# Second attention of an audio tower: exponentials taken from the score banks head by head, with the negated maximum as bias

## The reference, cut to what matters

```
q = (v @ WQ).reshape(B, S, H, C)
k = (v @ WK).reshape(B, S, H, C)
val = (v @ WV).reshape(B, S, H, C)
scores = jnp.einsum('bshc,bthc->bsth', q, k) * SCALE
A = jax.nn.softmax(scores, axis=2)
u = jnp.einsum('bsth,bthc->bshc', A, val).reshape(B, S, H * C)
return u @ Wout + bout
```

## Time and profile before

| | us |
|---|---|
| median of 3 runs | 961.59 (961.02 to 964.46) |
| the profiled execution, its own time | 963.74 |
| its span, first to last instruction | 962.0 |
| TensorE busy | 914.2 |
| VectorE busy | 703.5 |
| ScalarE busy | 639.6 |
| GpSimd busy | 520.0 |
| first scores of the second attention to its last | 583.46 to 848.13 |

### The profile page before, as it was taken

The page is one execution under the profiler, slowest core; times in us unless marked ns, Lnnn a source line. Parts: engine busy times, 40 slices in busy tenths (PEclk is TensorE's granted clock), DMA queues, the critical chain, the costliest instruction groups (busy, mean ns, idle before and its releaser), DMA issues. The chain is left out here.

```text
span 962.0 us, 35426 instructions
## 1 busy us (share of the span) xinstructions
PE 914.2 (95%) x12664; PEld 665.5 (69%) x12664; DVE 703.5 (73%) x1984; ACT 639.6 (66%) x1214; POOL 520.0 (54%) x815
## 2 busy tenths in 40 slices
PE   8899987999698999999999998999999999989998
PEld 3455655777476888888888884666666666558887
DVE  6677656777466668878878777988888888975553
ACT  2356566888567677868777776777777777743444
POOL 0010126887583687887878876555655556462110
PEclk9899998999899999999999999999999999999999
DMA  7533000000000000000000000000000000000001
GB/s 162 169 67 98 1 1 2 1 0 1 1 1 2 2 3 2 0 0 0 0 0 0 1 3 1 2 2 0 0 0 0 0 0 0 2 2 20 20 22 29
DMA packets 10657, 14.82 MB, mean 15 GB/s; under 512 B 8864, under 2 KB 9120, under 8 KB 9760
## 3 DMA queue, kind: packets, MB, share of 16 engines
q1 hardware_dynamic: 10400, 13.36, 5.7%
q10 hardware_dynamic: 192, 0.59, 0.2%
HBM read 11.85 MB, written 2.10 MB: 15 GB/s over the span
## 5 line engine op out<-in xcount | busy, mean ns | idle before, releaser
L1909 ACT ACTIVATE e_hid<-ps,cst 128x512 f32<-128x512 f32 x256 | 155.2, 689 | 53.0 <-PE ps L1671 53.0
L1606 POOL TENSOR_TENSOR e_acc<-e_acc,e_part 128x512 f32<-128x512 f32 x96 | 122.3, 1274 | 34.3 <-DVE e_part L1837 27.5
L1683 PEld LDWEIGHTS ps<-ew,e_hid 128*64 128x64 f32 x4096 | 124.8, 138 | 21.9 <-issue 10.4
L1683 PE MATMUL ps<-ew,e_hid 128*64 128x64 f32 x4096 | 133.8, 224 | 0.0
L1671 PE MATMUL ps<-e_xs,ew 64*128 64x256 f32 x1024 | 128.1, 389 | 0.7 <-ACT e_hid L1909 0.7
L1837 DVE TENSOR_TENSOR e_part<-ps,e_wt 128x512 f32<-128x512 f32 x128 | 86.8, 687 | 44.5 <-PE ps L1683 38.8
L1671 PEld LDWEIGHTS ps<-e_xs,ew 64*128 64x128 f32 x1024 | 93.5, 186 | 16.2 <-issue 3.1
L2114 POOL TENSOR_TENSOR a_sum<-a_part 128x256 f32<-128x256 f32 x64 | 47.0, 734 | 87.0 <-DVE a_part L2224 86.9
L2184 PEld LDWEIGHTS ps<-cst,a_ex 128*128 128x128 f32 x512 | 55.1, 140 | 49.1 <-issue 49.1
L2213 DVE TENSOR_REDUCE a_rmax<-ps 128x8 f32<-128x1024 f32 x64 | 78.2, 1222 | 14.8 <-PE ps L2176 13.5
L2216 DVE TENSOR_TENSOR a_diff<-ps,a_rmax 128x1024 f32<-128x1024 f32 x64 | 78.4, 1225 | 2.9
(11 more groups left out here) (275 smaller groups left out, 1986.4 us busy)
## 6 DMA issues: line engine op xcount, KB each, us to landing
x_in<-x_dram SPq DMA_DIRECT2D x12, 384.0 KB, 6.2
cst<-cst_dram SPq DMA_DIRECT2D x1, 3101.0 KB, 15.4
out_dram<-e_res SPq DMA_DIRECT2D x16, 128.0 KB, 2.0
ew<-ew_dram SPq DMA_DIRECT2D x1, 1024.0 KB, 8.5
x_in<-x_dram SPq DMA_DIRECT2D x5, 192.0 KB, 5.0
x_in<-x_dram ACTq DMA_DIRECT2D x3, 192.0 KB, 4.5
ew<-ew_dram SPq DMA_DIRECT2D x1, 512.0 KB, 9.3
cst<-cst_dram SPq DMA_DIRECT2D x1, 448.0 KB, 8.8
```

What stands on the lines that cost most here:

```text
L1606: eng.tensor_tensor(acc[:, :, :, :], acc[:, :, :, :], part[n % RING][:, :, :, :], ALU.add).then_inc(sum_sb.sem, 1)
L1683: mm = eng.matmul(m.ps[rows, 6 + n % 2, to:to + C], hid[e % 8][:, a:a + C], w2[:, e * C:e * C + C], start=True, stop=True)
L1909: nc.scalar.activation(hid[e % 8][:, :].rearrange("p (r t) -> p r t", r=2), m.ps[:, 4 - 2 * (n % 2):6 - 2 * (n % 2), j * 256:(j + 1) * 256 ...
```

## The change

The tile `diff` and its subtraction go. The maxima are written negated (`negate=True`), into two buffers in turn. ScalarE takes the exponential of each head by itself, straight from the score banks, with the head's negated maximum as bias: eight instructions of 128 x 128 elements in place of one of 128 x 1024. TensorE's next scores now wait for the last of these eight, where they waited for the subtraction. ScalarE's order of parts becomes `now, x0, lag1, x1, x2`: the exponentials stand ahead of the copy of the piece and of the copy of the transposed matrices, where they stood behind both.

```
-    rmax, rec = sb("rmax", [P, H]), sb("rec", [P, H])
+    nmax, rec = [sb(f"nmax{b}", [P, H]) for b in range(2)], sb("rec", [P, H])
...
         def now(g, b, s):
             if s == 0:
                 eng.wait_ge(uv_sb.sem, uv_sb.at(g, 2))
-                eng.wait_ge(diff_sb.sem, diff_sb.at(g - 1))
+                eng.wait_ge(exp_sb.sem, exp_sb.at(g - 1))
             else:
-                eng.wait_ge(diff_sb.sem, diff_sb.at(g, s))
+                eng.wait_ge(exp_sb.sem, exp_sb.at(g, H * s))
...
         def lag1(g, b, s):
             eng.wait_ge(prob_sb.sem, prob_sb.at(g, s) if s else prob_sb.at(g - 1))
-            eng.wait_ge(exp_sb.sem, exp_sb.at(g, s + 1))
+            eng.wait_ge(exp_sb.sem, exp_sb.at(g, H * (s + 1)))
...
-            eng.tensor_reduce(rmax[:, :], src, AX, ALU.max).then_inc(max_sb.sem, 1)
-            eng.wait_ge(max_sb.sem, max_sb.at(g, s + 1))
-            eng.wait_ge(exp_sb.sem, exp_sb.at(g, s) if s else exp_sb.at(g - 1))
-            eng.tensor_tensor(diff[:, :, :], src, bc(rmax[:, :], [P, H, P]), ALU.subtract).then_inc(diff_sb.sem, 1)
+            eng.tensor_reduce(nmax[s % 2][:, :], src, AX, ALU.max, negate=True).then_inc(max_sb.sem, 1)
...
         def now(g, b, s):
-            eng.wait_ge(diff_sb.sem, diff_sb.at(g, s + 1))
+            eng.wait_ge(max_sb.sem, max_sb.at(g, s + 1))
             eng.wait_ge(turn_ps.sem, turn_ps.at(g, s - 1) if s >= 2 else turn_ps.at(g - 1, s + 3))
-            nc.scalar.activation(ex[s % 2][:, :, :], diff[:, :, :], ACT.Exp).then_inc(exp_sb.sem, 1)
+            for j in range(H):
+                nc.scalar.activation(ex[s % 2][:, j, :], m.ps[:, 2 + j // 4, (j % 4) * P:(j % 4 + 1) * P], ACT.Exp,
+                                     bias=nmax[s % 2][:, j:j + 1]).then_inc(exp_sb.sem, 1)
...
-        rounds(eng, ("x0", "lag1", "x1", "now", "x2"), turned, piece, after=after, now=now, lag1=lag1)
+        rounds(eng, ("now", "x0", "lag1", "x1", "x2"), turned, piece, after=after, now=now, lag1=lag1)
```

More of the change, by code:

```diff
@@ L2018, in attention1 @@
     v = [sb(f"v{b}", [P, TS, H * V + W - V]) for b in range(2)]
-    diff = sb("diff", [P, H, P])
     ex = [sb(f"ex{b}", [P, H, P]) for b in range(2)]
     prob = [sb(f"prob{b}", [P, H, P]) for b in range(2)]
-    rmax, rec = sb("rmax", [P, H]), sb("rec", [P, H])
+    nmax, rec = [sb(f"nmax{b}", [P, H]) for b in range(2)], sb("rec", [P, H])
     part, sum4, sum2, sum1 = (sb(n, [P, k, C]) for n, k in (("part", H), ("sum4", 4), ("sum2", 2), ("sum1", 1)))
@@ L2027, in attention1 @@
     uv_ps, uv_sb = step("uv_ps", 4), step("uv_sb", 4)
-    score_ps, max_sb, diff_sb, exp_sb = step("score_ps", TS), step("max_sb", TS), step("diff_sb", TS), step("exp_sb", TS)
+    score_ps, max_sb, exp_sb = step("score_ps", TS), step("max_sb", TS), step("exp_sb", TS * H)
     turn_ps, prob_sb = step("turn_ps", TS), step("prob_sb", TS)
```

## The result

| | before | after |
|---|---|---|
| median, us | 962.7 (961.02 to 964.46, 4 runs) | 1023.19 (1022.6 to 1026.69, 4 runs) |
| span of the profiled execution, us | 962.0 | 1021.3 |

The changed kernel is slower: the ratio is 1.0621, with a 95% interval of 1.0592 to 1.0651. The forecast was 1021 us.

The account below looks back on a forecast made before the run. TensorE was taken to bound the old kernel, the score-bank circle the new: 48 x 4.72 + 15 x 6.49 = 323.9 us against 264.7, with start and end +59.4, giving 1021 us; range 1002 to 1048.

Parts of the forecast that it names:

- The circle of the banks: Score banks: scores, maximum, eight exponentials, then next scores; 4.72 us per sample, setting the pace alone.
- the slack: Score banks before the change: period 3.72 us against TensorE's 4.03 us in a slot with a piece, 0.3 us spare.
- The distance of two exponentials: ScalarE: successive exponentials start 0.257 us apart, so eight last 2.17 us.
- The rival with wider spacing: ScalarE: exponentials 0.294 to 0.35 us apart, adding 17 to 42 us, 1039 to 1063 us; 15 in 100.
- The estimate of 0.294: ScalarE: the skill's figures put exponentials 294 ns apart, eight lasting 2.45 us, result some 18 us later.
- The piece chain: Change of group: piece 3 waits for piece 2's copy behind the exponentials; step 6.49 us, 1.77 more, 15 times.
- The rival that the moved copies cost nothing: Slot 3 runs as any other, without a wait for piece 2's copy: +32.7, 994 us; 7 in 100.
- The sum: The stage's 63 steps: 48 x 4.72 + 15 x 6.49 = 323.9 us, against 264.7 before.
- the start: Start of the stage: ScalarE loads a table until 586.12, maxima ready at 585.8; +0.3 us.
- The clock: TensorE keeps the full clock in the stage; rival: it falls in pauses, up to +54, 1075 us; 5 in 100.
- In slots 1 and 2 that is harmless: Copies behind the exponentials: next piece's product starts 1.07 us after their end, the copy is seen done at 1.02.
- it does not get slower: Rival: VectorE held the bank circle more than TensorE; needs a circle of about 3.8 us, 966 us or less; 2 in 100.

Follow-up runs that it names:

- The run with sixteen: Changed kernel with sixteen exponentials of 128 x 64 elements in place of eight of 128 x 128: 1124.96 us, ratio 1.167.
- VectorE's copy: Changed kernel with the copy of piece 2 done by VectorE behind the maxima of slot 3: 1001.68 us, ratio 1.0386.
- the order run: Kernel before with ScalarE's new order of parts alone, subtraction and one exponential kept: 1021.35 us, ratio 1.0591.
- one exponential: Changed kernel with one exponential of 128 x 1024 straight from the banks, no bias, maximum not subtracted but still waited for: 974.04 us, ratio 1.0085.
- half of the new order: Kernel before with only the copies of the transposed matrices and of the turned input moved behind the exponential: 986.94 us, ratio 1.0219.

## Why the prediction was right

**The circle of the banks.** Forecast 0.11 + 1.18 + 1.26 + 2.17 = 4.72 us, measured 0.05 + 1.18 + 1.26 + 2.18 = 4.67. The term that was off is TensorE's start after ScalarE's end: 649.40 + 2.18 = 651.58, and 651.63. I had taken 0.11 from a wait ahead of transposes. The scores waited for exponentials 34 times, 29.4 us in all, and not nearly once a sample: ahead of a step across groups the wait falls on piece 3, and in slot 1 TensorE itself is hardly done before the exponentials are.

What I said of the slack, 0.3 us a sample, holds for the slots with a piece alone. In slot 0 the step before was 3.61 us, and the circle was as long, 1.08 + 1.25 + 1.28 = 3.61:

```profile
636.71 1.23 DVE L2213 TENSOR_REDUCE a_rmax<-ps 128x8 f32<-128x1024 f32 x1 [0.45 <-PE ps L2176]
...
637.96 1.23 DVE L2216 TENSOR_TENSOR a_diff<-ps,a_rmax 128x1024 f32<-128x1024 f32 x1
```

So slot 0 paid the whole lengthening, 4.56 less 3.61, 0.95 us, and slots 1 and 2 paid 0.64. The sum doesn't depend on this, as it was set against the measured 264.7.

**The distance of two exponentials.** Forecast 0.257, measured (2.18 - 0.383)/7 = 0.257. The run with sixteen gives the same per-instruction part of 0.15 us. The rival with wider spacing is out (the lower end of its times should read 1038 us, not 1039). The estimate of 0.294 from the figures of the Trainium skill (ScalarE: Activation LUTs, What ACT_TABLE_LOAD costs) is above the measured distance; the length of one by the same figures, 387 ns, agrees with the mean of 383.

**The piece chain.** Forecast 6.49 us from exponentials' end to exponentials' end, measured 6.44; VectorE's copy took out 22.6 us of the time. The rival that the moved copies cost nothing is out.

**The sum.** Forecast 323.9 us from first to last scores; measured from these two rows, 324.7:

```profile
582.49 1.02 PE L2175 MATMUL ps<-a_u,a_xs 64*128 64x512 f32 x4
...
907.23 1.13 PE L2175 MATMUL ps<-a_u,a_xs 64*128 64x512 f32 x4 [1.05 <-ACT a_ex L2266]
```

Two errors cancel here, which is luck. A steady group takes 20.44 us and not 20.65, some 3 us over the stage. Against that, the start, which I gave 0.3 us, costs about as much: the first two groups take 3.2 us more than steady ones. TensorE pauses there, and the granted clock is 0.66 over these 10 us:

```profile
583.00:593.00 10.00, 6.79 (x25) 3.18 (x21) 4.47 (x13) 7.02 (x20) 5.79 (x12) 0.66 0.00 0
```

**The clock.** In the steady stage it stayed at full rate, as I forecast. The rival is real all the same: in two of the experiments, whose ordinary steps were 5.88 and 6.27 us, it came.

**What the forecast left out.** It followed the copies of the pieces, and not ScalarE's copy of the turned input, which now stands behind the exponentials too. "In slots 1 and 2 that is harmless" holds only under the long circle. The turned input's copy behind the exponentials would cost by itself nearly what the circle costs in slots 0 and 1: two steps of 9.3 us in the order run (646.62 to 655.90), 9.2 in the changed kernel (647.07 to 656.30). So the loss can't be split into so much for the eight exponentials and so much for the order. With the new order both work through one quantity: the time from the scores' start to the end of the exponentials. It is 1.18 + 1.26 + 1.26 + 1.06 = 4.76 us in the order run, 4.62 in the changed kernel and 3.47 with one exponential, and their medians are 1021, 1023 and 974. With the old order the subtraction gave the banks back, and the copies of pieces 0 to 2 and of the turned input stood ahead of the exponential, so its 4.76 cost nothing; with half of the new order nearly the same time cost 2.2%. That a single quantity rules is read from these runs; no run varies it alone. The rival "it does not get slower" was priced too low for the same reason: with one exponential the circle was 3.5 us, under its 3.8, and the kernel still took 974 us, not 966. Its slots of 3.8 us are also shorter than the 4.03 that TensorE needs with a piece.

## What to carry to other kernels

Before an operation is dropped because its engine has room, ask what it sets free. Here a subtraction of 1.2 us released a PSUM bank pair that exists once; the work that took its place as the last reader was 2.2 us long, and 0.64 to 0.95 us was paid for every sample. Cutting one activation into eight costs 0.15 us for each added instruction, and all of that counts on a circle through a single buffer. And a reordered queue has to be followed through each thing moved behind, down to the small copies: one of 0.6 us made a step 1.6 us longer once a group in the order run.

## What the runs showed of the hardware

The granted clock of TensorE stayed at 1.00 in the steady stage of the changed kernel, where TensorE was busy for 168 of 200 us and its pauses were 1.7 us at most. It was 0.90 and 0.92 over 300 us in the old order with eight exponentials (busy for 216, waiting 2.17 us ahead of most scores) and with sixteen exponentials (busy for 218, waiting up to 2.64 us). There the medians were 41 and 26 us above what I had worked out at full clock. A copy of 128 x 1024 that stands in ScalarE's queue behind the eight short activations, or behind another such copy, is listed at 1.07 to 1.09 us and starts 0.16 us before the end of what it follows, where it is listed at 1.026 in the kernel before. It ends 0.91 to 0.92 us after that, as the forecast had it, so only its listed start is earlier.
